# A one-core graph layer on Trainium2: a constant projection transposed in the head, a tile turned inside an accumulation, and a last tile finished in halves

## The chip, the cores and the metric

The kernel runs on one core of a Trainium2 chip. The metric is the device time of one execution in microseconds (us). The core has TensorE (PE, matmuls and transposes into PSUM), VectorE (DVE), ScalarE (ACT), GpSimd (POOL) and SyncE (SP, which only issues DMAs here). ACT and POOL issue some DMAs too. Each engine has its own instruction list, worked off in order; the lists meet only at semaphores.

## The reference

```
h   = relu(layernorm(x))                      # x: 1250 x 512, f32
xn  = batchnorm(h) * g1 + b1
agg = segment_sum(xn[src], dst) / max(deg, 1) # 20000 edges
conv = relu(agg @ W_conv + b_conv)
q, k, v = h @ Wq, h @ Wk, h @ Wv on the first 256 rows, 8 heads of 64
u = (t * scale) @ proj.T                      # proj: 256 x 64, for q and for k
qf, kf = exp(u - diag - max) / 16 + 1e-6
attn = (qf @ (kf.T @ v)) / (qf @ sum(kf)) @ Wo
out = x + batchnorm(conv + attn + h) * g2 + b2
```

## The kernel before, in words

The 1250 rows are ten tiles of 128 (the last has 98), the 512 features four tiles f = 0 to 3. Each engine's order is written out by hand. Eight PSUM banks are given out by two lists, `order` and `order_end`: `pe_open` takes the next name of the list, gives it a bank and waits until that bank's last user has been read; `full` and `landed` are "PE has written it", `read` and `stored` are "it has been read".

**Head (0 to about 27 us).** SP and ACT issue the loads of x, of the edges and of the weights. PE first runs `rouse(18)`, eighteen matmuls on constant ones whose result nobody reads, then `edge_search(0)` (tiny matmuls that count edges, L807), the transposes of h tiles 1 and 0 (L637), one more rouse, `edge_search(1)`, and the matmuls of q (L645). After the transposes of tiles 2 to 5 it runs `project_consts()`: two transposes of the projection `pj` (L818) and one of `vrow`, the five vectors g1, b1, g2, b2, b_conv (L819). Its loads are the last that SP issues before it waits for x tile 7 (L326, L328). DVE copies the result to `pT` and `vec` in `constants()` (L1143, L1144), after the statistics of x and the first piece of batch statistics. On ACT the head is: three x loads (L429), a table load with a first square root (L431), the standard deviation of the first group (L426), h tile 0, the copies of the transposed h tiles 1 and 0 (L389), and then the second group.

**Middle (to 118 us).** Attention, one-hot edge counts, and G = xn @ W_conv (L715), which is split into two f16 parts gh and gl. `uncovered_edges()` loads a flag into PE's registers and branches on it.

**End.** `aggregate(f, c)` (L992) sums gh and gl over ten source tiles s for one column chunk: 20 matmuls. For f = 0 to 2 the chunks are 512, 512 and 226 columns, for f = 3 they are 376, 376, 214, 156 and 128. For each chunk DVE runs `y(f, c)` (L1407, L1412, statistics L1414); after the last chunk `moments` and `scale` give one scale and shift per feature, and ACT scales the tile (L619), as three blocks j. PE turns (transposes) each block (`transpose_z`, L1020), DVE adds x to it (`finish`, L1442), and SP stores it (L345, L349). For f = 2 the blocks 0 and 2 are turned by `turn_with_residual` (x is added by PE, ACT copies the result), and block 1 by `transpose_z` with an add on DVE, all after the last chunk of f = 3. For f = 3 DVE scales block 0 itself (L1461), ACT the rest as 256, 256 and 226 columns; the store of block 1 is issued by ACT (L623), the others by SP.

Of the kernel before, what the change touches and what calls it, by code (L numbers as in the profile page):

```python
# [14 lines left out]
P = 128  # L15
# [26 lines left out]
NPAD = NT * P  # L42
SLOW_LINKS = 8
SEARCHED = 2
ROUSE, ROUSE_NEXT = 18, 1
EP, EJ = 125, E // 125
# [6 lines left out]
def chunks_of(f):  # L53
    return CHUNKS if f < FT - 1 else LAST_CHUNKS


def rows_of(i):
    return P if i < NT - 1 else LAST


def gnn_kernel(nc, x, src, dst, g1, b1, g2, b2, w_conv, b_conv, w_q, w_k, w_v, w_o, proj, out):
    with ExitStack() as ctx:
# [3 lines left out]
        def sem(name):  # L66
# [124 lines left out]

        order = [("first",), ("hT", 1), ("hT", 0), ("q", 0), ("q", 1), ("hT", 2), ("hT", 3), ("hT", 4), ("hT", 5),
# [8 lines left out]
        for f in range(1, FT - 1):  # L201
            order_end += [("agg", f, 0), ("agg", f, 1)] + [("zT", f - 1, j) for j in range(3)] + [("agg", f, 2)]
        order_end += [("agg", FT - 1, c) for c in range(len(LAST_CHUNKS))] + [("zT", FT - 2, j) for j in (0, 2, 1)]
        order_end += [("zT", FT - 1, j) for j in range(3)]
        uses = {}
# [103 lines left out]
        @block.sync  # L309
        def _(sp):  # L310
            def load_x(i):
                sp.dma_start(xs[0:rows_of(i), i, :], x[i * P:i * P + rows_of(i), :]).then_inc(x_in[i], 16)

            load_x(0)
            sp.dma_start(edst[:, :], dst.rearrange("(p j) -> p j", p=EP)).then_inc(dst_in, 16)
            wq_rows = w_q.rearrange("(t p) n -> p t n", p=P)
            sp.dma_start(wq[:, :, 0:2 * P], wq_rows[:, :, 0:2 * P]).then_inc(wq_in[0], 16)
            load_x(2)
            load_x(4)
            sp.dma_start(wq[:, :, 2 * P:D], wq_rows[:, :, 2 * P:D]).then_inc(wq_in[1], 16)  # L320
            for i in (6, 7, 8, 9):
                if i == NT - 1:
                    sp.wait_ge(pad_zero, 1)
                load_x(i)
            for k, v in enumerate((g1, b1, g2, b2, b_conv)):
                sp.dma_start(vrow[4 * k:4 * k + 4, :], v.rearrange("(t p) -> t p", p=P)).then_inc(vec_in, 16)  # L326
            for k in range(2):
                sp.dma_start(pj[:, :, k * DH:(k + 1) * DH], proj.rearrange("(t p) d -> p t d", p=P)).then_inc(pj_in, 16)  # L328
            sp.wait_ge(x_in[7], 16)
            sp.dma_start(wk, w_k.rearrange("(t p) n -> p t n", p=P)).then_inc(wk_in, 16)  # L330
            sp.dma_start(wc[:, :, :], w_conv.rearrange("(t p) n -> p t n", p=P)).then_inc(wc_in, 16)
            sp.dma_start(wvo[:, :, :], w_v.rearrange("(t p) n -> p t n", p=P)).then_inc(wv_in, 16)
            for t in range(AT):
                landed(sp, "v", t)
            sp.dma_start(wvo[:, :, :], w_o.rearrange("(t p) n -> p t n", p=P)).then_inc(wo_in, 16)
            sp.dma_start(esrc[:, :], src.rearrange("(p j) -> p j", p=EP)).then_inc(src_in, 16)
            landed(sp, "agg", 0, 0)
            for i in range(NT):
                load_x(i)
            for f in range(FT):  # L340
                c = slice(f * P, (f + 1) * P)
                for j in {FT - 2: (0, 2, 1), FT - 1: (0, 2)}.get(f, (0, 1, 2)):
                    stored(sp, "zT", f, j)
                    if j < 2:
                        sp.dma_start(out[512 * j:512 * (j + 1), c].rearrange("(t p) n -> p t n", p=P),  # L345
                                     xs[:, 4 * j:4 * (j + 1), c]).then_inc(o_out, 16)
# [4 lines left out]
            sp.wait_ge(o_out, 16 * 4 * FT)  # L351

# [31 lines left out]
        def _(act):  # L384
# [42 lines left out]

            for i in (1, 3, 5):
                act.dma_start(xs[:, i, :], x[i * P:(i + 1) * P, :]).then_inc(x_in[i], 16)  # L429
            act.wait_ge(cst_set, 7)  # L430
# [4 lines left out]
            store_hT(1, ACT.Relu)  # L435
            store_hT(0)
            ln_std_of(1)
            act.wait_ge(ln_ready, 2)
# [182 lines left out]
            c = slice((FT - 1) * P, D)  # L621
            stored(act, "zT", FT - 1, 1)
            act.dma_start(out[512:1024, c].rearrange("(t p) n -> p t n", p=P), xs[:, 4:8, c]).then_inc(o_out, 16)  # L623
# [3 lines left out]
        def _(pe):  # L627
# [133 lines left out]

            def uncovered_edges():
                pe.wait_ge(flag_ready, 1)
                covered = pe.value_load(flag[0:1, 0:1], min_val=0, max_val=1)
                with pe.If(covered == 0):
# [90 lines left out]

            rouse(ROUSE)
            edge_search(0)
            pe.wait_ge(id_set, 1)
            transpose_h(1)  # L860
# [12 lines left out]
            transpose_h(5)  # L873
            project_consts()
            pe.wait_ge(wk_in, 16)
# [102 lines left out]
            for i in range(2):  # L978
                stored(pe, "attnT", i)
            heads_out(0)  # L980
            heads_out(1)
            uncovered_edges()
            assert counts[0] == NGRP

            def aggregate(f, c):
                c0, cn = chunks_of(f)[c]
                pe.wait_ge(group_stored, -(-(c0 + cn) // (GW * W)))
                acc = pe_open(pe, "agg", f, c)
                for s in range(NT):
                    n = rows_of(s)  # L990
                    for gg in (gh, gl):
                        last = nc.tensor.matmul(acc[:, 0:cn], gg[0:n, s, f * P:(f + 1) * P], A16[0:n, s, c0:c0 + cn],  # L992
                                                start=(s == 0 and gg is gh), stop=(s == NT - 1 and gg is gl))
                last.then_inc(full("agg", f, c), 1)
# [12 lines left out]
            def transpose_z(f, parts=(0, 1, 2)):  # L1007
                for j in parts:
                    acc = pe_open(pe, "zT", f, j)
                    if f < FT - 1:  # L1010
                        pe.wait_ge(z_act, 3 * f + j + 1)
                    elif j == 0:
                        pe.wait_ge(z_dve, 1)
                    elif j == 2:
                        pe.wait_ge(z_act, 3 * f + 3)
                    for i in range(4 * j, min(4 * j + 4, NT)):
                        if f == FT - 1 and i in (4, 6):
                            pe.wait_ge(z_act, 3 * f + i // 2 - 1)
                        o = (i - 4 * j) * P
                        last = nc.tensor.transpose(acc[:, o:o + P], yT[:, f, i * P:(i + 1) * P], ident[:, :])  # L1020
                    last.then_inc(full("zT", f, j), 1)
# [18 lines left out]
            turn_with_residual(FT - 2, 2)  # L1040
            transpose_z(FT - 2, (1,))
            transpose_z(FT - 1)


        @block.vector
        def _(dve):
# [94 lines left out]
            def constants():  # L1141
                acc = landed(dve, "consts")
                V.tensor_copy(pT[:, :], acc[:, 0:M])  # L1143
                V.tensor_copy(vec[:, :], acc[:, M:M + 20]).then_inc(read("consts"), 1)  # L1144
                stored(dve, "consts")
# [241 lines left out]
            def last_phase(slow):  # L1387
# [47 lines left out]
                def finish(f, j):  # L1435
                    a, b = 4 * j, min(4 * j + 4, NT)
# [17 lines left out]
                f = FT - 1  # L1454
                for c in range(len(LAST_CHUNKS) - 1):
                    y(f, c)
# [3 lines left out]
                dve.wait_ge(st2_ready, FT)  # L1460
                V.tensor_scalar(yT[:, f, 0:512], yT[:, f, 0:512], s2[:, f:f + 1], t2[:, f:f + 1],  # L1461
                                ALU.mult, ALU.add).then_inc(z_dve, 1)
                finish(f - 1, 1)
                for j in range(3):
                    finish(f, j)
# [79 lines left out]
```

## Time and profile before

| what | value |
|---|---|
| median of 3 runs | 175.11 us (174.8 to 175.3) |
| the profiled execution, its own time | 174.95 us |
| its span, first to last instruction | 173.1 us |
| mean granted TensorE clock | 0.992 |
| busy: PE, DVE, ACT, POOL | 166.0, 138.3, 89.8, 7.6 us |

The profiled time is 1.85 us above its span; that part lies outside the instructions. A matmul's busy time overlaps its neighbours', so PE's 166.0 us say that it was never long without work, not that it ran at its peak.

### The profile page before, as it was taken

The numbers are of one execution on the slowest core, as the hardware profiler recorded it, in microseconds if no ns is written. First come the engines' busy times: TensorE is split into PE (matmuls) and PEld (weight loads), VectorE is DVE, ScalarE is ACT, GpSimd is POOL, SyncE is SP. The second block draws the span as 40 slices with busy tenths as digits, with TensorE's granted clock in tenths as the row PEclk, the third lists the DMA queues.
The fourth block names the chain that finished last, engine by engine and source line by source line (L and its number), as shares of the span: only waits on it lengthen the run. The fifth ranks groups of instructions, "written<-read, shape, count | busy, mean of one in ns | idle before, by whom it ended". The sixth has DMA issues, their size and how long they took to land.

```text
span 173.1 us, 3035 instructions
## 1 busy us (share of the span) xinstructions
PE 166.0 (96%) x1135; PEld 109.6 (63%) x1136; DVE 138.3 (80%) x317; ACT 89.8 (52%) x163; POOL 7.6 (4%) x22
## 2 busy tenths in 40 slices
PE   7999999999999999999999999999999999999980
PEld 2588887545545546557767797684464574777960
DVE  3987989899947786999656785976999998597980
ACT  3228998749793789969506164218600505004060
POOL 5047000000000000000000000000000000000000
PEclk9999999999999999999999999999999999999996
DMA  5999960000800000000000000000395004050046
GB/s 169 353 342 284 310 221 0 0 4 0 251 12 0 4 0 0 0 4 2 0 4 0 0 4 0 0 4 4 94 315 187 0 27 121 6 146 2 0 118 183
DMA packets 12412, 13.71 MB, mean 79 GB/s; under 512 B 1474, under 2 KB 7788, under 8 KB 12396
## 3 DMA queue, kind: packets, MB, share of 16 engines
q1 hardware_dynamic: 11116, 12.18, 22.4%
q10 hardware_dynamic: 960, 1.05, 1.8%
q0 software_dynamic: 320, 0.26, 0.7%
q8 instruction: 11, 0.18, 0.4%
q14 instruction: 5, 0.04, 0.1%
HBM read 10.92 MB, written 2.56 MB: 78 GB/s over the span
## 4 chain that ended last, share of the span: by engine, by line
PE 88%; DVE 6%; ACT 2%; issue 1%; DVEq 0%; ACTq 0%
PE bank L992 22%; PE bank L715 20%; PE bank L645 8%; PE bank L666 4%; PE bank L739 4%; PE bank L729 4%; PE bank L758 4%; PE bank L797 4%; PE bank L692 4%; PE bank L657 3%; PE bank L637 3%; PE bank L703 2%; PE bank L1020 2%; DVE r L1412 1%; DVE r L1407 1%
## 5 line engine op out<-in xcount | busy, mean ns | idle before, releaser
L992 PE MATMUL bank<-r,gh 128*128 128x512 f16 (+8 forms) x140 | 39.3, 314 | 0.0
L992 PE MATMUL bank<-r,gl 128*128 128x512 f16 (+8 forms) x140 | 39.3, 313 | 0.0
L715 PE MATMUL bank<-wc,xs 128*128 128x512 f32 (+1 forms) x80 | 38.5, 608 | 0.2 <-DVE gl L1243 0.2
L1100 DVE TENSOR_TENSOR ohb<-iota,bcol 128x1280 f16<-128x1280 f16 x25 | 20.5, 819 | 3.7 <-PE bank L657 3.7
L715 PEld LDWEIGHTS bank<-wc,xs 128*128 128x128 f32 (+1 forms) x80 | 13.6, 187 | 11.6 <-issue 11.6
L398 ACT ACTIVATE r<-bank 128x500 f16<-128x500 f32 x25 | 18.3, 765 | 3.4 <-PE bank L657 3.4
L992 PEld LDWEIGHTS bank<-r,gh 128*128 128x128 f16 (+1 forms) x140 | 13.5, 97 | 8.5 <-issue 0.3
L992 PEld LDWEIGHTS bank<-r,gl 128*128 128x128 f16 (+1 forms) x140 | 13.6, 97 | 8.2
L613 ACT ACTIVATE bw<-mv,epst 128x1 f32<-128x1 f32 x4 | 1.2, 295 | 31.0 <-DVE mv L1418 31.0
L645 PE MATMUL bank<-hT,r 128*128 128x256 f32 x64 | 14.6, 383 | 0.0
L657 PEld LDWEIGHTS bank<-ohv,ohb 128*128 128x128 f16 x250 | 9.7, 98 | 6.6 <-issue 5.3
L521 ACT ACTIVATE gh<-bank 128x512 f16<-128x512 f32 (+1 forms) x10 | 6.0, 601 | 14.6 <-PE bank L715 14.6
L645 PEld LDWEIGHTS bank<-hT,r 128*128 128x128 f32 x64 | 11.9, 189 | 2.0 <-issue 0.4
L1243 DVE SCALAR_TENSOR_TENSOR gl<-bank,gh 128x512 f16<-128x512 f32 (+1 forms) x10 | 6.9, 688 | 5.2 <-ACT gh L521 5.2
L1407 DVE SCALAR_TENSOR_TENSOR r<-bank,cinv,r 128x512 f32<-128x512 f32 (+5 forms) x14 | 8.2, 584 | 3.3 <-PE bank L992 3.2
L1100 DVE TENSOR_TENSOR ohv<-iota,vcol 128x500 f16<-128x500 f16 x25 | 10.3, 413 | 0.0
L657 PE MATMUL bank<-ohv,ohb 128*128 128x50 f16 x250 | 10.3, 184 | 0.0
L619 ACT ACTIVATE r<-r,t,s 128x512 f32<-128x512 f32 (+2 forms) x12 | 7.5, 689 | 3.0 <-DVE t L1432 3.0
L1412 DVE SCALAR_TENSOR_TENSOR r<-r,nb,hT 128x512 f32<-128x512 f32 (+5 forms) x14 | 8.3, 591 | 0.5
L729 PEld LDWEIGHTS bank<-v,r 128*128 128x128 f32 x64 | 7.6, 192 | 1.0 <-issue 1.0
L797 PE MATMUL bank<-cone 128*128 128x512 f16 x19 | 6.9, 536 | 1.2 <-DVE cone L1062 1.2
L1393 DVE RECIPROCAL r<-r 128x1250 f32<-128x1250 f32 x1 | 8.0, 7967 | 0.1
(179 smaller groups left out, 269.1 us busy)
## 6 DMA issues: line engine op xcount, KB each, us to landing
xs<-in_x SPq DMA_DIRECT2D x15, 256.0 KB, 5.0
out<-xs SPq DMA_DIRECT2D x7, 256.0 KB
r<-in_L_gnn_Wq SPq DMA_DIRECT2D x2, 512.0 KB, 7.2
r<-in_L_gnn_Wk SPq DMA_DIRECT2D x1, 1024.0 KB, 5.6
wc<-in_L_gnn_W_conv SPq DMA_DIRECT2D x1, 1024.0 KB, 9.6
wvo<-in_L_gnn_Wv SPq DMA_DIRECT2D x1, 1024.0 KB, 12.8
wvo<-in_L_gnn_Wo SPq DMA_DIRECT2D x1, 1024.0 KB, 5.2
xs<-in_x ACTq DMA_DIRECT2D x3, 256.0 KB, 4.4
```

What stands on the lines that cost most here:

```text
L398: act.activation(A16[:, :, p * GW * W:(p + 1) * GW * W].rearrange("p a (q d) -> p q a d", q=GW), bank[p % 2][:, 0:GW * NT * W].rearrange(" ...
L619: act.activation(yT[:, f, a:b], yT[:, f, a:b], ACT.Identity, bias=t2[:, f:f + 1], scale=s2[:, f:f + 1]).then_inc(z_act, 1)
L645: last = nc.tensor.matmul(acc[:, t * NA:(t + 1) * NA], w[:, f, c:c + P], hT[:, f, 0:NA], start=(f == 0), stop=(f == FT - 1))
L657: last = nc.tensor.matmul(bank[p % 2][:, q * NT * W:(q + 1) * NT * W], ohb[:, s, :], ohv[:, s, :], start=True, stop=True)
L715: last = nc.tensor.matmul(acc[0:n, :], xnT[:, f, i * P:i * P + n], wc[:, f, :], start=(f == 0), stop=(f == FT - 1))
L729: last = nc.tensor.matmul(acc[:, j * (DH + 1):(j + 1) * (DH + 1)], kf[:, t, h, m * P:(m + 1) * P], v1[:, t, h, :], start=(t == 0), stop=(t ...
L797: nc.tensor.matmul(bank[0][:, :], cone[:, :], cone[:, 0:1].to_broadcast([P, 512]), start=True, stop=True)
L992: last = nc.tensor.matmul(acc[:, 0:cn], gg[0:n, s, f * P:(f + 1) * P], A16[0:n, s, c0:c0 + cn], start=(s == 0 and gg is gh), stop=(s == NT ...
L1100: last = V.tensor_tensor(oh[:, s0:s0 + n, :].rearrange("p s (m t) -> p s m t", t=2), iota16[:, 0:size].rearrange("p (m t) -> p m t", t=2). ...
L1393: link(V.reciprocal(rdeg[:, :], rdeg[:, :]))
L1407: V.scalar_tensor_tensor(out=yT[:, f, c0:c0 + cn], in0=sums, scalar=cinv[:, f:f + 1], in1=rdeg[:, c0:c0 + cn], op0=ALU.mult, op1=ALU.mult) ...
L1412: link(V.scalar_tensor_tensor(out=yT[:, f, c0:c0 + cn], in0=yT[:, f, c0:c0 + cn], scalar=nb[:, f:f + 1], in1=hT[:, f, c0:c0 + cn], op0=ALU ...
```

## The change

It moves the projection's transposes to the head of PE's list and turns the rest around them, and it rearranges the end of f = 2 and f = 3.

- **Head.** `rouse` runs 15 instead of 18 matmuls; `project_consts()` follows at once, ahead of `edge_search(0)`. Its loads (five of `vrow`, two of `pj`) are issued by ACT behind x tile 1; x tiles 3 and 5 go to SP's queue, ahead of 2 and 4. ACT copies the result to `pT` and `vec` behind the copy of h tile 0; DVE's two copies go.
- **Bank lists.** `consts` is first in `order`; block 1 of f = 2 stands between chunks 1 and 2 of f = 3 in `order_end`, and f = 3 has four blocks.
- **Flag.** The load of the flag into PE's registers stands ahead of `heads_out(1)`, the branch stays.
- **Block 1 of f = 2** is turned inside chunk 1 of f = 3, ahead of source tile 7; DVE adds x to it between chunks 0 and 1, and SP stores it first of the three.
- **f = 3** has the blocks (0, 2), (2, 4), (4, 8), (8, 10) in tiles: DVE scales, PE turns, DVE finishes and SP stores the first 512 columns as two halves.

```diff
-ROUSE, ROUSE_NEXT = 18, 1
+TURN_AT = 7
+ROUSE, ROUSE_NEXT = 15, 1
+def tiles_of(f, j):
+    if f < FT - 1:
+        return 4 * j, min(4 * j + 4, NT)
+    return ((0, 2), (2, 4), (4, 8), (8, NT))[j]
...
-        order = [("first",), ("hT", 1), ("hT", 0), ("q", 0), ("q", 1), ("hT", 2), ("hT", 3), ("hT", 4), ("hT", 5),
-                 ("consts",), ("k", 0), ...
+        order = [("consts",), ("first",), ("hT", 1), ("hT", 0), ("q", 0), ("q", 1), ("hT", 2), ("hT", 3), ("hT", 4), ("hT", 5),
+                 ("k", 0), ...
-        order_end += [("agg", FT - 1, c) for c in range(len(LAST_CHUNKS))] + [("zT", FT - 2, j) for j in (0, 2, 1)]
-        order_end += [("zT", FT - 1, j) for j in range(3)]
+        order_end += [("agg", FT - 1, c) for c in range(2)] + [("zT", FT - 2, 1)]
+        order_end += [("agg", FT - 1, c) for c in range(2, len(LAST_CHUNKS))]
+        order_end += [("zT", FT - 2, j) for j in (0, 2)]
+        order_end += [("zT", FT - 1, j) for j in range(4)]
...  # SP
-            load_x(2)
-            load_x(4)
+            for i in (3, 5, 2, 4):
+                load_x(i)
-            for k, v in enumerate((g1, b1, g2, b2, b_conv)):
-                sp.dma_start(vrow...)
-            for k in range(2):
-                sp.dma_start(pj...)
-                for j in {FT - 2: (0, 2, 1), FT - 1: (0, 2)}.get(f, (0, 1, 2)):
+                for j in {FT - 2: (1, 0, 2), FT - 1: (0, 1, 3)}.get(f, (0, 1, 2)):
...  # ACT
-            for i in (1, 3, 5):
-                act.dma_start(xs[:, i, :], ...)
+            act.dma_start(xs[:, 1, :], ...)
+            for k, v in enumerate((g1, b1, g2, b2, b_conv)):
+                act.dma_start(vrow...)
+            for k in range(2):
+                act.dma_start(pj...)
             store_hT(0)
+            acc = landed(act, "consts")
+            act.activation(pT[:, :], acc[:, 0:M], ACT.Copy)
+            act.activation(vec[:, :], acc[:, M:M + 20], ACT.Copy).then_inc(read("consts"), 1)
...  # PE
             rouse(ROUSE)
+            pe.wait_ge(id_set, 1)
+            project_consts()
             edge_search(0)
-            project_consts()
             heads_out(0)
+            pe.wait_ge(flag_ready, 1)
+            covered = pe.value_load(flag[0:1, 0:1], min_val=0, max_val=1)
             heads_out(1)
                 for s in range(NT):
+                    if (f, c, s) == (FT - 1, 1, TURN_AT):
+                        transpose_z(FT - 2, (1,))
             turn_with_residual(FT - 2, 2)
-            transpose_z(FT - 2, (1,))
-            transpose_z(FT - 1)
+            transpose_z(FT - 1, (0, 1, 2, 3))
...  # DVE
-                V.tensor_copy(pT[:, :], acc[:, 0:M])
-                V.tensor_copy(vec[:, :], acc[:, M:M + 20]).then_inc(read("consts"), 1)
+                y(f, 0)
+                finish(f - 1, 1)
+                for c in range(1, len(LAST_CHUNKS) - 1):
                     y(f, c)
-                V.tensor_scalar(yT[:, f, 0:512], ...)
-                finish(f - 1, 1)
-                for j in range(3):
+                for a in (0, 256):
+                    V.tensor_scalar(yT[:, f, a:a + 256], ...).then_inc(z_dve, 1)
+                for j in range(4):
                     finish(f, j)
```

## Rows read from the trace of the kernel before

**Rows 1.** The page: the chain that ended last, shares of the span by engine

```profile
PE 88%; DVE 6%; ACT 2%; issue 1%; DVEq 0%; ACTq 0%
```

**Rows 2.** The chain in order of time, the head (start us, us, what)

```profile
1.21 6.56 PE bank L797 x18
7.77 0.18 PE bank L807 x4
...
9.97 7.02 PE bank L645 x32
...
18.73 0.22 PE bank L818 x2
...
19.12 3.65 PE bank L645 x16
```

**Rows 3.** Windows of L797: stretch, length, PE and PEld busy, PEclk, DMA share, GB/s

```profile
1.20:5.80 4.60, 4.59 (x11) 1.65 (x12) 1.00 0.81 250
6.30:7.60 1.30, 1.30 (x7) 0.49 (x5) 1.00 1.06 384
```

**Rows 4.** Timeline of ACT, head (start us, us, instruction, idle before)

```profile
0.76 1.39 ACTq L429 DMA_DIRECT2D xs<-in_x  x3
2.18 1.28 ACT L431 ACT_TABLE_LOAD   x1 [2.18 <-issue]
...
5.58 0.29 ACT L426 ACTIVATE lnw<-mv,epst 128x2 f32<-128x2 f32 x1 [1.90 <-DVE mv L1072]
...
12.21 0.30 ACT L426 ACTIVATE lnw<-mv,epst 128x4 f32<-128x4 f32 x1 [2.64 <-DVE mv L1072]
```

**Rows 5.** L429, ACT's three loads of x: from issue to landing

```profile
DMA to landing us min/median/max: 3.5/4.4/6.4
```

**Rows 6.** Timeline of SP's queue: the last vector load and both projection loads

```profile
7.32 0.29 SPq L326 DMA_DIRECT2D vrow<-in_L_gnn_b_conv  x1
7.66 0.91 SPq L328 DMA_DIRECT2D pj<-in_L_gnn_proj  x2
```

**Rows 7.** L328, the two projection loads: from issue to landing

```profile
DMA to landing us min/median/max: 6.4/6.8/7.2
```

**Rows 8.** Timeline of DVE, head: statistics of x tiles 3 and 5; copy to pT

```profile
8.52 1.28 DVE L1068 BATCH_NORM_STATS2 st<-xs 128x6 f32<-128x512 f32 x2
...
21.07 0.41 DVE L1143 COPY pT<-bank 128x256 f32<-128x256 f32 x1
```

**Rows 9.** L764, the flag load on PE's sequencer (duration ns, start us)

```profile
L764 PEldq TENSOR_LOAD <-flag x1: 486/486/486, 113.5 to 113.5; - x1
```

**Rows 10.** The chain in order of time, from the turn of f = 1 on

```profile
149.59 1.09 PE bank L1020 x10
...
166.09 0.56 DVE r L1461
```

**Rows 11.** Timeline of DVE, end: chunk 1 of f = 3; the last adds

```profile
159.04 0.61 DVE L1407 SCALAR_TENSOR_TENSOR r<-bank,cinv,r 128x376 f32<-128x376 f32 x1 [1.02 <-PE bank L992]
...
167.44 1.62 DVE L1442 TENSOR_TENSOR xs<-bank,xs 128x512 f32<-128x512 f32 x3 [0.21 <-PE bank L1020]
```

**Rows 12.** L1442, DVE's four last adds (ns min/median/max)

```profile
L1442 DVE TENSOR_TENSOR xs<-bank,xs x4: 416/683/692, 166.5 to 168.7; 128x512 f32<-128x512 f32 x3, 128x256 f32<-128x256 f32 x1
```

**Rows 13.** Timeline of ACT, end: the scalings of f = 2 and f = 3

```profile
156.31 1.99 ACT L619 ACTIVATE r<-r,t,s 128x512 f32<-128x512 f32 x3 [1.00 <-DVE t L1432]
...
166.38 1.55 ACT L619 ACTIVATE r<-r,t,s 128x256 f32<-128x256 f32 x3
```

**Rows 14.** Timeline of SP's queue, end

```profile
167.36 1.18 SPq L345 DMA_DIRECT2D out<-xs  x2
169.09 0.84 SPq L349 DMA_DIRECT2D out<-xs  x2
```

**Rows 15.** Windows, end: length; PE, PEld, DVE, ACT, POOL busy, PEclk, DMA share, GB/s

```profile
168.50:169.50 1.00, 0.00 (x0) 0.00 (x0) 0.57 (x2) 0.00 (x0) 0.00 (x0) 1.00 0.99 284
...
170.50:171.50 1.00, 0.00 (x0) 0.00 (x0) 0.00 (x0) 0.00 (x0) 0.00 (x0) 0.50 0.95 253
```

More of the change, by code:

```diff
@@ L324, in _ @@
                 load_x(i)
-            for k, v in enumerate((g1, b1, g2, b2, b_conv)):
-                sp.dma_start(vrow[4 * k:4 * k + 4, :], v.rearrange("(t p) -> t p", p=P)).then_inc(vec_in, 16)
-            for k in range(2):
-                sp.dma_start(pj[:, :, k * DH:(k + 1) * DH], proj.rearrange("(t p) d -> p t d", p=P)).then_inc(pj_in, 16)
             sp.wait_ge(x_in[7], 16)
@@ L341, in _ @@
                 c = slice(f * P, (f + 1) * P)
-                for j in {FT - 2: (0, 2, 1), FT - 1: (0, 2)}.get(f, (0, 1, 2)):
+                for j in {FT - 2: (1, 0, 2), FT - 1: (0, 1, 3)}.get(f, (0, 1, 2)):
                     stored(sp, "zT", f, j)
-                    if j < 2:
-                        sp.dma_start(out[512 * j:512 * (j + 1), c].rearrange("(t p) n -> p t n", p=P),
-                                     xs[:, 4 * j:4 * (j + 1), c]).then_inc(o_out, 16)
+                    a, b = tiles_of(f, j)
+                    if b < NT:
+                        sp.dma_start(out[a * P:b * P, c].rearrange("(t p) n -> p t n", p=P), xs[:, a:b, c]).then_inc(o_out, 16)
                     else:
@@ L350, in _ @@
             sp.wait_ge(src_in, 16)
-            sp.wait_ge(o_out, 16 * 4 * FT)
+            sp.wait_ge(o_out, 16 * (4 * FT + 1))
         @block.gpsimd
@@ L426, in ln_std_of @@
                 act.activation(lnw[:, 1, a:b], mv[:, a:b, 1], ACT.Sqrt, bias=epst[:, 0:1]).then_inc(ln_std, 1)
-            for i in (1, 3, 5):
-                act.dma_start(xs[:, i, :], x[i * P:(i + 1) * P, :]).then_inc(x_in[i], 16)
+            act.dma_start(xs[:, 1, :], x[P:2 * P, :]).then_inc(x_in[1], 16)
+            for k, v in enumerate((g1, b1, g2, b2, b_conv)):
+                act.dma_start(vrow[4 * k:4 * k + 4, :], v.rearrange("(t p) -> t p", p=P)).then_inc(vec_in, 16)
+            for k in range(2):
+                act.dma_start(pj[:, :, k * DH:(k + 1) * DH], proj.rearrange("(t p) d -> p t d", p=P)).then_inc(pj_in, 16)
             act.wait_ge(cst_set, 7)
@@ L621, in _ @@
             c = slice((FT - 1) * P, D)
-            stored(act, "zT", FT - 1, 1)
+            stored(act, "zT", FT - 1, 2)
             act.dma_start(out[512:1024, c].rearrange("(t p) n -> p t n", p=P), xs[:, 4:8, c]).then_inc(o_out, 16)
@@ L760, in heads_out, with uncovered_edges @@
                 last.then_inc(full("ha", i), 1)
-            def uncovered_edges():
-                pe.wait_ge(flag_ready, 1)
-                covered = pe.value_load(flag[0:1, 0:1], min_val=0, max_val=1)
+            def uncovered_edges(covered):
                 with pe.If(covered == 0):
@@ L857, in _ @@
             rouse(ROUSE)
+            pe.wait_ge(id_set, 1)
+            project_consts()
             edge_search(0)
-            pe.wait_ge(id_set, 1)
             transpose_h(1)
@@ L980, in _ @@
             heads_out(0)
+            pe.wait_ge(flag_ready, 1)
+            covered = pe.value_load(flag[0:1, 0:1], min_val=0, max_val=1)
             heads_out(1)
-            uncovered_edges()
+            uncovered_edges(covered)
             assert counts[0] == NGRP
@@ L1008, in transpose_z @@
                 for j in parts:
+                    a, b = tiles_of(f, j)
                     acc = pe_open(pe, "zT", f, j)
@@ L1011, in transpose_z @@
                         pe.wait_ge(z_act, 3 * f + j + 1)
[L1012 to L1017, printed above, removed]
+                    elif j < 2:
+                        pe.wait_ge(z_dve, j + 1)
+                    for i in range(a, b):
+                        if f == FT - 1 and i in (4, 6, 8):
                             pe.wait_ge(z_act, 3 * f + i // 2 - 1)
-                        o = (i - 4 * j) * P
+                        o = (i - a) * P
                         last = nc.tensor.transpose(acc[:, o:o + P], yT[:, f, i * P:(i + 1) * P], ident[:, :])
@@ L1141, in constants @@
             def constants():
-                acc = landed(dve, "consts")
-                V.tensor_copy(pT[:, :], acc[:, 0:M])
-                V.tensor_copy(vec[:, :], acc[:, M:M + 20]).then_inc(read("consts"), 1)
                 stored(dve, "consts")
@@ L1435, in finish @@
                 def finish(f, j):
-                    a, b = 4 * j, min(4 * j + 4, NT)
+                    a, b = tiles_of(f, j)
                     c = slice(f * P, (f + 1) * P)
@@ L1454, in last_phase @@
                 f = FT - 1
-                for c in range(len(LAST_CHUNKS) - 1):
+                y(f, 0)
+                finish(f - 1, 1)
+                for c in range(1, len(LAST_CHUNKS) - 1):
                     y(f, c)
@@ L1460, in last_phase @@
                 dve.wait_ge(st2_ready, FT)
-                V.tensor_scalar(yT[:, f, 0:512], yT[:, f, 0:512], s2[:, f:f + 1], t2[:, f:f + 1],
-                                ALU.mult, ALU.add).then_inc(z_dve, 1)
-                finish(f - 1, 1)
-                for j in range(3):
+                for a in (0, 256):
+                    V.tensor_scalar(yT[:, f, a:a + 256], yT[:, f, a:a + 256], s2[:, f:f + 1], t2[:, f:f + 1],
+                                    ALU.mult, ALU.add).then_inc(z_dve, 1)
+                for j in range(4):
                     finish(f, j)
```

2 rows, old and new, of the table order are left out of this document.

## The prediction, on record before the changed kernel ran

> **What bounds the kernel now.** I read the chain that ended last first, because it says whose time counts. PE holds 88% of it [rows 1]. Followed in order of time, the chain stays on PE from 1.21 us nearly without a hole through the head [rows 2], and it leaves PE for DVE only when the second chunk of f = 3 lands at 159.04 [rows 11]. From there DVE's work on the chunks, the scale and the last blocks sets the end [rows 10, 11], and behind it the stores. So a PE instruction in the head or in the aggregation counts in full, a DVE or ACT instruction before 159 us counts only if PE waits for it, and after 159.04 it is the other way round. Then I read ACT's, DVE's and SP's timelines in the head [rows 4, 6, 8] and the landings of their loads [rows 5, 7], since the change makes PE wait for loads that have long landed today. Last come the end's timelines [rows 11, 13, 14] and the DMA engines' share there [rows 15].
>
> **Head, what goes.** Three rousing matmuls go. The first eleven take 4.6 us, so 0.42 us apart; in the stretch from 6.3 us on seven records fill 1.3 us, under 0.22 us apart [rows 3]: that is PE at 1.2 GHz and then at 2.4 GHz, and it rose after some five microseconds of rousing. The three that go are fast ones: 18 took 6.56 us, 15 end at 1.21 + 6.56 - 3 x 0.217 = 7.12 us. The three transposes of the constants took 19.12 - 18.73 = 0.39 us on the path [rows 2]. They are moved, not removed: their place at 18.73 closes up by 0.39 us and the head opens by as much. Without a wait, then, the head is 0.65 us shorter and all of it reaches the end of PE's unbroken chain.
>
> **Head, the wait that is added.** PE now stands still until all five vector loads and both projection loads have landed, and behind the waiting instruction are both edge searches, the h transposes and the q matmuls; behind those, ACT's copies of h and DVE's first_rows, with the gathers that POOL issues after it. When do the loads land? ACT issues x tile 1 at 0.76; one x load takes 0.46 us of its queue [rows 4]. A vector load takes 0.29 and a gap of 0.05, a projection load 0.46 [rows 6]. So the five vectors are issued from 1.22 to 2.92, the projection at 2.92 and 3.38. How long a load needs from issue to landing depends on what is ahead of it: 3.5 us for the first x on ACT's queue, 4.4 for the second, 6.4 for the third [rows 5], 6.4 and 7.2 for the projection itself behind SP's whole list [rows 7]. The bounds for the second projection load are thus 3.38 + 3.5 = 6.9 us and 3.38 + 7.2 = 10.6 us. Its case is nearest to the second x on ACT's queue, one large transfer ahead and the bus shared with SP's: 3.38 + 4.4 = 7.8 us. PE then waits from 7.12 to 7.8; with 0.05 us to wake and 0.39 us of transposes, edge_search(0) starts at 8.24 where it started at 7.77 [rows 2]. That is 0.47 us late, minus the 0.39 us at 18.73: **the head costs 0.08 us** (bounds: -0.65 with the landing by 7.1, and 10.6 + 0.05 + 0.39 - 7.77 - 0.39 = +2.9 with the latest).
>
> The second x of ACT's queue, issued at 1.2, landed 4.4 us later [rows 4, 5]: its own queue didn't spare it the traffic. The Trainium skill, "DMA: Bandwidth & Descriptors", section "Issuing engines are not separate DMA queues", says as much: DMAs of all issuers run on the same 16 engines and interleave, and a second issuer saves issue time only. By it the move to ACT buys no bandwidth, and the projection's wait must be read from loads that ran in the same crowd.
>
> **Head, the edits that I cost at nothing.** ACT's issues end at about 3.85 instead of 2.15, its table load of 1.28 us [rows 4] at 5.2 and the first square root at 5.4; the standard deviation is wanted at 5.58. The cover is only 0.2 us thick; without it, the first group's scale is late by as much. ACT's two new copies, some 0.4 and 0.2 us, fall into its 2.64 us of idle time before 12.21 [rows 4]. DVE loses about 0.5 us of copies at 21.07 [rows 8], but PE waited for nothing of DVE's there, so this is slack and not time. x tiles 3 and 5 now queue behind half of Wq on SP; DVE wants them from 8.52 on [rows 8], and since the same bytes are on the same engines in another order, I expect them by about 8. If one were late, tiles 2 to 5 of h would be. The third place is the k matmuls, which follow at once where the constants stood: their weights wait for x tile 7, but no longer behind seven small loads. The flag's load was done at 113.5, under the matmuls that PE still had queued [rows 9]; the load wasn't what PE waited for at the branch, so moving it gives nothing.
>
> **End, the turn inside the chunk.** Ten transposes of f = 1 took 1.09 us between two chunks [rows 10], so four take 0.44. They stand ahead of chunk 1's last six matmuls, and DVE idles 1.02 us for that chunk before 159.04 [rows 11]. So the landing moves to 159.48 and everything behind it, in full: **+0.44 us**. Their operand is ready in time: ACT's second block of f = 2 is done two thirds into 156.31 + 1.99 [rows 13], near 157.8, and source tile 7 of the chunk comes up at about 157.9. DVE's added add (0.68 us [rows 12]) fits between chunk 0 and the 159.48. What is taken away at the end is worth little: the turn ran while DVE scaled, and the add while PE turned block 0; DVE idled 0.21 us even so [rows 11].
>
> **End, the halves.** The scale of 512 columns takes 0.56 us [rows 10], so half some 0.35; PE starts 0.2 us earlier and turns two blocks instead of four, 0.22 us less, and DVE's first add can start near 167.0 instead of 167.44. But ACT's three scalings end at 166.38 + 1.55 = 167.93 [rows 13] whatever DVE does, and the last two adds hang on them: the 128x512 add starts perhaps 0.08 us earlier, the last (416 ns [rows 12]) follows it. **-0.07 us** (bounds 0 and -0.15, the last add's start at 168.65 against 167.93 and 0.57 us for wake-up and two transposes).
>
> **End, the stores.** SP issues the store of block 1 of f = 2 at 167.36 [rows 14] in the middle of the last rush; after, it goes out near 160. The DMA engines are full in that rush (share 0.99 at 284 GB/s, 0.95 at 253 [rows 15]), and 256 KB are 0.92 us of their time. SP's last issue starts near 169.48 and ends at 169.93 [rows 14]; the span ends at 173.1. An unloaded 256 KB load takes 3.5 us, of which 0.9 are its bytes, so a small one needs some 2.6; the last store's 3.1 leave about 0.5 to gain, and the one ACT issues just before it has its queue freed too. I take **-0.6 us** (bounds 0, if latency alone sets the end, and -0.92). One more SP issue falls between 167.4 and 169.0, where SP has nothing else.
>
> **Sum.** 174.95 + 0.08 + 0.44 - 0.07 - 0.6 = 174.80 us for the profiled execution. That one is 0.16 us under the median of the three runs, so the median to expect is 174.96, say 174.9. Less than 0.3% (0.53 us) either way is about what a measurement of this kernel can't tell from no change.
>
> **The rivals.** (a) The projection lands early. If it is there by 7.1, PE never waits and the head gives its whole 0.65 us: 175.11 - 0.65 - 0.23 = 174.2. For it: ACT's queue has only one x ahead of the projection, and 128 KB are half of one x tile. Against: the share of the bus it got in its neighbours' time. Any landing under 7.4 us makes the kernel faster by over 0.3%. (b) The other side: the projection is late. Its pieces are small, and its own loads took 6.4 and 7.2 us [rows 7]; at a landing of 8.8 us the head costs 1.08 us and the kernel takes 176.0; at the 6.4 us of the third x [rows 5] it is 9.8 us and 176.9. It decides from 8.5 us on. (c) PE's idle time costs the clock: PE rose to 2.4 GHz only shortly before the wait begins [rows 3], and at the end of the kernel, idle after its last transposes, it is granted 0.50 by 170.5 [rows 15]. If it fell in the new gap, rousing it again at 0.42 instead of 0.22 us a matmul would cost about 12 x 0.2 = 2.4 us: 177.5. The gap of 0.7 us is shorter than what preceded that fall, 2 us. The Trainium skill, "TensorE: Matmul & The Clock Gate", section "HAM oscillation — how this bites in real kernels", warns of just this: PE that waits for a DMA between bursts drops to the low clock. (d) The stores gain nothing: 175.5, still no change.
>
> **Chances.** My forecast with (d), within 0.3%: 0.41. (a), faster: 0.37. (b) 0.18 and (c) 0.04, slower: 0.22. The range: down to 173.9, where (a) and the full 0.92 us of the stores meet (175.11 - 0.65 - 0.55); up to 176.0, where (b) has its middle price; (c) and the far half of (b) are left out.
>
> **What would show it.** In the profile after: 15 rousing matmuls ending at 7.1, and PE's idle time ahead of L818, 0 (a), 0.7 (mine) or over 1.3 us (b); the granted clock and the spacing of the q matmuls; q's start against 9.97; the k matmuls' start; DVE's wait for chunk 1 with 0.44 us more on the clock than the head's shift; the last add; and the time from SP's last issue to the end of the span, 3.1 before and some 2.5 after. I would be wrong by another way if x tile 3 or 5 came late for DVE, or if ACT's table load pushed the first square root beyond 5.6.

## The result, and the profile after

The changed kernel takes **183.75 us** (median of 4 runs, 183.61 to 184.04), against 175.11 us before: ratio **1.050, interval 1.048 to 1.052**. I had predicted 174.9 us and given slower a chance of 0.22. The profiled execution took 183.61 us with a span of 180.9 us, 7.8 us longer than before. Its time outside the span is 2.7 us where it was 1.85. This part isn't the change's doing as far as the runs show: in the changed kernel's own executions it lay between 2.0 and 2.8 us, in the unchanged kernel's later ones between 1.8 and 2.3, and in those of a kernel with only the flag's load moved up to 2.9. So the spans are compared below. The changed kernel's other executions have spans of up to 182.0 us and lower granted clocks (0.956 to 0.965, against the profiled 0.971), so the account below holds for the profiled one.

The page of the kernel after (busy time, the granted clock in 40 slices, the chain by engine):

```profile
PE 169.6 (94%) x1133; PEld 112.2 (62%) x1133; DVE 138.5 (77%) x317; ACT 90.0 (50%) x165; POOL 7.6 (4%) x22
...
PEclk9955799999999999999999999999999999999999
...
PE 83%; DVE 6%; DMA 5%; ACT 2%; ACTq 2%; issue 1%; DVEq 0%
```

Before, no DMA was named in the chain's shares [rows 1]; now one has 5% of it, and the clock is down to a half in slices 3 and 4. The timeline of PE in the head and the chain through the same stretch say which DMA it is (after; start us, us):

```profile
1.21 5.99 PE L806 MATMUL bank<-cone 128*128 128x512 f16 x15 [1.21 <-DVE cone L1073]
11.97 0.66 PE L827 MATMUL bank<-ident,pj 128*128 128x128 f32 x2 [4.77 <-DMA pj<-in_L_gnn_proj]
```

```profile
3.68 8.16 DMA pj<-in_L_gnn_proj
...
11.97 0.66 PE bank L827 x2
12.63 0.22 PE bank L828
12.85 0.52 PE bank L816 x4
13.37 1.81 PE bank L648 x8
15.18 0.43 PE bank L806
15.60 1.60 PE bank L816 x16
17.21 8.51 PE bank L656 x32
25.72 1.75 PE bank L648 x16
...
125.70 0.53 PE bank L1038 x3
126.23 19.33 PE bank L1005 x100
```

PE stood still for 4.77 us: the second projection load, issued at 3.68, landed 8.16 us later at 11.84. And what follows is slow. The eight transposes of h take 1.81 us (0.93 before), sixteen edge matmuls 1.60 (0.87), the 32 matmuls of q 8.51 instead of 7.02 [rows 2]. Windows of the kernel after (stretch, length, PE, PEld, DVE, ACT, POOL busy, PEclk, DMA share, GB/s):

```profile
7.20:9.80 2.60, 0.00 (x0) 0.00 (x0) 2.55 (x4) 0.51 (x1) 0.00 (x0) 1.00 1.07 375
10.00:12.00 2.00, 0.03 (x1) 0.06 (x1) 0.00 (x0) 0.00 (x0) 0.00 (x0) 0.50 1.10 359
12.00:17.00 5.00, 5.00 (x32) 4.37 (x33) 0.00 (x0) 1.55 (x4) 0.00 (x0) 0.50 0.71 219
17.00:20.00 3.00, 3.00 (x9) 2.46 (x10) 2.25 (x11) 0.30 (x1) 1.56 (x2) 0.50 1.01 372
20.20:22.00 1.80, 1.80 (x10) 1.58 (x9) 1.73 (x6) 1.22 (x2) 1.50 (x2) 1.00 1.03 397
```

PE went idle at 7.20. The clock was still granted in full at 9.8, was at 0.50 (1.2 GHz) from 10.0, and stayed there for eight more microseconds after PE was busy again, until 20.1.

**The account of the span.** The first transpose of the constants stands where edge_search(0) stood: it starts 11.97 - 7.77 = 4.20 us later. That is the wait of 4.77 us, less the 0.57 us by which rousing ended earlier (7.20 against 7.77). The transposes' own 0.39 us are only moved to the front, away from 18.73. From there to the end of q's matmuls PE took 25.72 - 11.97 = 13.75 us; before, the same instructions took 0.39 + (16.99 - 7.77) = 9.61 us, so the low clock cost +4.14. Then it comes back in steps. The aggregation begins 7.66 us late (126.23 against 118.57): of the 8.34 us, the flag's load takes back 0.5 and the first k matmuls, 3.46 us instead of 3.65, 0.2. DVE's wait for chunk 1 ends 8.20 late (+0.54, the turn), DVE's last add 8.13 late (-0.07), the span 7.8 (-0.3, the stores).

### The profile page after: what moved, and what is told of

It is laid out like the page before. It is cut to its first block, busy times and chain, and to the rows that moved or that the text cites. A ratio compares the mean times of both kernels' runs of the same rounds, so it can differ in the third digit from the quotient of the medians.

```text
span 180.9 us, 3034 instructions
## 1 busy us (share of the span) xinstructions
PE 169.6 (94%) x1133; PEld 112.2 (62%) x1133; DVE 138.5 (77%) x317; ACT 90.0 (50%) x165; POOL 7.6 (4%) x22
## 4 chain that ended last, share of the span: by engine, by line
PE 83%; DVE 6%; DMA 5%; ACT 2%; ACTq 2%; issue 1%; DVEq 0%
PE bank L1005 21%; PE bank L726 19%; PE bank L656 9%; DMA pj<-in_L_gnn_proj 5%; PE bank L677 4%; PE bank L750 4%; PE bank L740 4%; PE bank L769 4%; PE bank L703 4%; PE bank L668 3%; PE bank L648 3%; PE bank L1032 2%; PE bank L714 2%; PE bank L816 1%; ACTq L435 1%; DVE r L1420 1%
## 5 line engine op out<-in xcount | busy, mean ns | idle before, releaser
L726 PEld LDWEIGHTS bank<-wc,xs 128*128 128x128 f32 (+1 forms) x80 | 13.6, 187 | 11.6 <-issue 11.6
L1005 PEld LDWEIGHTS bank<-r,gl 128*128 128x128 f16 (+1 forms) x140 | 13.6, 97 | 8.1
L656 PE MATMUL bank<-hT,r 128*128 128x256 f32 x64 | 16.0, 409 | 0.0
L656 PEld LDWEIGHTS bank<-hT,r 128*128 128x128 f32 x64 | 13.0, 207 | 2.4 <-issue 0.4
L394 ACT ACTIVATE hT<-bank 128x512 f32<-128x512 f32 (+1 forms) x10 | 5.2, 590 | 8.7 <-PE bank L648 8.7
## 6 DMA issues: line engine op xcount, KB each, us to landing
wvo<-in_L_gnn_Wv SPq DMA_DIRECT2D x1, 1024.0 KB, 10.9
```

The costliest lines, as they stand in the source:

```text
L656: last = nc.tensor.matmul(acc[:, t * NA:(t + 1) * NA], w[:, f, c:c + P], hT[:, f, 0:NA], start=(f == 0), stop=(f == FT - 1))
L726: last = nc.tensor.matmul(acc[0:n, :], xnT[:, f, i * P:i * P + n], wc[:, f, :], start=(f == 0), stop=(f == FT - 1))
```

## Experiments

Each ran beside the kernel before on the same chip; the ratios are against that. They are the record's, each with its 95% interval, and can differ from the quotient of the two medians by 0.1 to 0.2%. "Span" and the lines shown are the profiled execution's.

### The end's part alone

```diff
 # head as in the kernel before; kept of the change:
+                    if (f, c, s) == (FT - 1, 1, TURN_AT):
+                        transpose_z(FT - 2, (1,))
...  # the halves of f = 3, the stores' order, the flag's load ahead of heads_out(1)
```

> The kernel before with the end's part of the change and the flag's load moved, the head untouched. Theory 1, the whole loss is in the head: 174.8 us, from 175.11 with -0.5 (the flag: in the profile after, the gap ahead of the degree matmuls is gone), +0.54 (the four transposes inside chunk 1), -0.07 and -0.3 (stores). Theory 2, the 0.85 us by which the changed kernel's time grew beyond its span comes from the end: 175.6 us.

Measured: 174.73 us against 175.45, ratio **0.997 (0.995 to 0.998)**, span 172.8. So the loss is in the head, and the end's part with the flag is a small gain. DVE's end (timeline of this run):

```profile
158.39 0.69 DVE L1451 TENSOR_TENSOR xs<-bank,xs 128x512 f32<-128x512 f32 x1 [0.61 <-PE bank L1030]
159.35 0.61 DVE L1416 SCALAR_TENSOR_TENSOR r<-bank,cinv,r 128x376 f32<-128x376 f32 x1 [0.27 <-PE bank L1003]
...
167.40 1.91 DVE L1451 TENSOR_TENSOR xs<-bank,xs 128x256 f32<-128x256 f32 x4 [0.27 <-PE bank L1030]
```

The add that was moved (158.39) fits into the hole ahead of chunk 1, as predicted. From the start of the aggregation (118.34 here, 118.57 before) to chunk 1 on DVE it is 41.01 us against 40.47: +0.54.

### The constants' transposes back in their old place, loads still on ACT

```diff
-            pe.wait_ge(id_set, 1)
-            project_consts()
             edge_search(0)
+            pe.wait_ge(id_set, 1)
...
             transpose_h(5)
+            project_consts()
```

> The changed kernel with the constants' transposes and their copies on ACT back behind the transposes of h tile 5; the loads stay on ACT's queue, ROUSE stays 15. Theory 1, PE's wait for the loads and what it does to the clock is the loss: 174.2 us (174.8 less three rousing matmuls, 0.65), q starts near 9.4. Theory 2, the loads' new order on the queues (x tiles 3 and 5 on SP, small loads on ACT) costs by itself: 176 us or more.

Measured: 175.47 against 175.45, ratio 1.001 (0.998 to 1.004), span 173.5; two of its ten executions took 178.8 and 179.1 us, with a granted clock of 0.984. In the profiled one the wait and the low clock are gone, so waiting for these loads in this place makes the loss. But it is 1.3 us above my 174.2 (0.9 if the kernel before is taken at the 175.45 measured beside it), and its span is 0.7 us longer than that of the end's part alone, which has three rousing matmuls more. PE's and ACT's timelines and the chain show where that goes:

```profile
1.21 4.73 PE L806 MATMUL bank<-cone 128*128 128x512 f16 x15 [1.21 <-DVE cone L1073]
...
7.84 1.06 PE L648 MATMUL bank<-ident,xs 128*128 128x128 f32 x8 [1.54 <-DVE xs L1118]
...
19.89 0.48 PE L656 MATMUL bank<-hT,r 128*128 128x256 f32 x1 [0.75 <-DMA r<-in_L_gnn_Wk]
```

```profile
5.85 0.28 ACT L431 ACTIVATE lnw<-mv,epst 128x2 f32<-128x2 f32 x1
```

```profile
6.05 8.33 DMA xs<-in_x
14.38 0.02 issue
14.40 5.44 DMA r<-in_L_gnn_Wk
```

The h transposes cannot start before DVE has scaled x tile 1 (L1118), so removing three rousing matmuls saves nothing: q's matmuls start at 9.85, against 9.83 before. Here this scale is itself late. ACT's seven small issues push its table load back, the standard deviation starts at 5.85 instead of 5.5, and the transposes start at 7.84, against 7.58 in the end's part alone. That is the danger the prediction named for ACT's edits, at 0.25 us. And x tile 7 lands at 14.4, so SP issues Wk later than before (12.48), and PE waits 0.75 us for it. How much of that delay is the small loads' doing isn't shown: over all profiled executions SP issued Wk at 12.5 to 13.8 us with the head's loads as before, and at 13.0 to 14.4 with the changed ones, and in the split kernel further below, with no vector ahead of the x tiles, at 13.6.

### Rousing until the projection lands

```diff
-ROUSE, ROUSE_NEXT = 15, 1
+ROUSE, ROUSE_NEXT = 37, 1
```

> The changed kernel with 37 rousing matmuls instead of 15, so that PE works until the projection lands near 11.9 us. Theory 1, the loss has two parts, 4.85 us of waiting and 4.15 us of work at the low clock behind it: 179.6 us, with q's first 32 matmuls back at 7.0 us. Theory 2, the low clock is not the gap's doing: 183.7 us.

Measured: 178.93 us, ratio **1.019 (1.017 to 1.022)**, span 177.1. The projection lands as late as before (12.02), and 22 more matmuls whose result nobody reads buy back 3.8 us of span. They end at 10.9; the gap of 1.24 us that is left doesn't lower the clock. The chain of this run:

```profile
12.02 0.14 issue
12.15 0.41 PE bank L827 x2
...
13.05 0.93 PE bank L648 x8
...
15.07 7.02 PE bank L656 x32
```

Same landing, same instructions, full clock: 9.9 us from 12.15 to 22.09 where the changed kernel took 13.75. So the long gap brings the low clock, and that is about half of the loss of span.

### The projection ahead of the vectors on ACT's queue

```diff
-            for k, v in enumerate((g1, b1, g2, b2, b_conv)): act.dma_start(vrow...)
             for k in range(2): act.dma_start(pj...)
+            for k, v in enumerate((g1, b1, g2, b2, b_conv)): act.dma_start(vrow...)
```

> The changed kernel with the two projection loads issued ahead of the five vector loads on ACT's queue. Theory 1, the five small loads in front are what keeps the projection's first packet back: the projection is in by 8.5 us and PE waits for the vectors at the latest until 10, 178 to 181 us. Theory 2, the share of the bus is the cause: the last landing stays at 11.8 us and the time at 183.7 us.

Measured: four executions from 175.93 to 181.34 us, too unlike for a ratio; granted clock 0.994 in the shortest and 0.964 in the longest, which is the profiled one (span 178.8). Its tile view has the projection at 3.9 and 5.4 us from issue to landing, so it was in at 7.1. The vectors, 2 KB each and the last of them issued at 3.9, kept PE until 9.15:

```profile
9.15 0.66 PE L827 MATMUL bank<-ident,pj 128*128 128x128 f32 x2 [2.42 <-DMA vrow<-in_L_gnn_b_conv]
```

Theory 1 holds for the landing. The profiled execution works at half the clock from 9.0 to 19.1. The granted clocks suggest that this kernel loses the clock in some executions and not in others, which goes with the spread of 5 us; only the one trace shows it.

### The same with rousing until the vectors land

```diff
-ROUSE, ROUSE_NEXT = 15, 1
+ROUSE, ROUSE_NEXT = 27, 1
```

> The changed kernel with the projection loads ahead of the vectors' (as in the run with that order) and 27 rousing matmuls instead of 15, so that PE is busy until the last vector lands near 9.1 us. Theory 1, the low clock comes from the gap even at 2.4 us: 176.3 us (174.7 for the end's part, +1.9 for the later start of the edge search, -0.39 for the closed place), all runs alike. Theory 2, the gap alone is the cost and 2.4 us do not lower the clock: no better than 180 us.

Measured: 176.75 us (176.44 to 177.07), ratio 1.008 (1.006 to 1.011), span 175.0; PE busy in all 13 us from 7 to 20, clock 1.00. The spread is gone with the gap. Rousing went on until 10.12, about 1 us longer than the vectors would have asked. q starts at 12.85, 2.9 us late, and the kernel is 1.3 us over the one before.

### The constants split: the projection alone in the head

```diff
             act.dma_start(xs[:, 1, :], ...)
-            for k, v in enumerate((g1, b1, g2, b2, b_conv)): act.dma_start(vrow...)   # back to SP, behind x tile 9
             for k in range(2): act.dma_start(pj...)
...
             transpose_h(5)
+            turn_vectors()   # the transpose of vrow; DVE copies it to vec
```

> The changed kernel with the constants split: only the projection is loaded on ACT's queue behind x tile 1 and turned in the head; the five vector loads go back to SP's queue, where they were, and their transpose back behind h tile 5 (ACT no longer copies it, DVE does). Theory 1, the five small loads are what holds the projection and PE up: the projection lands by 7.5 us, PE waits under 0.5 us, the clock stays up, ratio 0.996 to 1.002. Theory 2, the projection's own small pieces on a full bus are slow: it lands after 9 us and the ratio is over 1.02.

Measured: 175.04 against 175.40, ratio 1.000 (0.997 to 1.002), span 173.2; one of its twelve executions took 179.75 us, with a granted clock of 0.98. PE's timeline, and the tile view of the projection:

```profile
1.22 4.98 PE L805 MATMUL bank<-cone 128*128 128x512 f16 x15 [1.22 <-DVE cone L1077]
7.80 0.41 PE L825 MATMUL bank<-ident,pj 128*128 128x128 f32 x2 [1.60 <-DMA pj<-in_L_gnn_proj]
...
19.60 2.64 PE L655 MATMUL bank<-hT,r 128*128 128x256 f32 x11 [0.27 <-DMA r<-in_L_gnn_Wk]
```

```profile
DMA to landing us min/median/max: 3.9/4.9/6.0
```

Without the five vector loads the projection is in at 7.7 us, not 11.84, and the loss is gone. It was issued at 1.7 and took 6.0 us to land. PE still idles 1.6 us (here the clock had risen early and rousing ended at 6.2), and in this execution the clock stayed. But a projection in the head is worth nothing either: its ratio is no better than that of the end's part alone (0.995 to 0.998). Whether it is worse isn't shown, since the intervals overlap.

### What ten kilobytes in front of the projection do

Two runs on the split kernel. One puts x tile 3 (256 KB), taken from SP's queue, between x tile 1 and the projection on ACT's queue, the other one vector (2 KB); the other four vectors stay with SP.

```diff
             act.dma_start(xs[:, 1, :], ...)
+            act.dma_start(xs[:, 3, :], ...)        # first run; SP then loads x tiles 5, 2, 4
+            act.dma_start(vrow[0:4, :], g1...)     # second run
             for k in range(2): act.dma_start(pj...)
```

> The run with the split constants (vectors back on SP's queue), with x tile 3 moved from SP's queue to ACT's, between x tile 1 and the projection: 256 KB in front of the projection in the place where the changed kernel has 10 KB in five loads. Theory 1, it is the number of small loads that holds ACT's ring, not their bytes: the projection lands earlier than the changed kernel's 11.84 us, near 9 us, and PE waits some 2.5 us. Theory 2, the bytes in front and the full bus set it: 11 us or later.

> The run with the split constants, with one of the five vector loads (g1, 2 KB) on ACT's queue between x tile 1 and the projection. Theory 1, each small load holds the ring by itself: the projection lands near 8.5 us, a fifth of the way from 7.7 (no vector in front) to 11.84 (five). Theory 2, only the sum of issue times counts, 0.35 us a load: 8.0 us.

Measured: 180.72 us, ratio 1.031 (1.027 to 1.036), with the tile; 178.30 us, 1.018 (1.014 to 1.021), with one vector. PE's timelines, first the run with the tile, then that with one vector:

```profile
9.71 0.66 PE L826 MATMUL bank<-ident,pj 128*128 128x128 f32 x2 [3.05 <-DMA pj<-in_L_gnn_proj]
```

```profile
9.74 0.66 PE L826 MATMUL bank<-ident,pj 128*128 128x128 f32 x2 [2.68 <-DMA pj<-in_L_gnn_proj]
```

| in front of the second projection load, behind x tile 1 | issued | landed | issue to landing |
|---|---|---|---|
| nothing (split) | 1.7 us | 7.7 us | 6.0 us |
| x tile 3, 256 KB | 2.2 | 9.6 | 7.4 |
| one vector, 2 KB | 2.2 | 9.6 | 7.4 |
| five vectors, 10 KB (the changed kernel) | 3.7 | 11.84 | 8.2 |

Each row is one profiled execution; the changed kernel's landing came back at 12.02 in the run with 37 rousing matmuls. Bytes don't set it: 2 KB hold the projection back as much as 256 KB do, 1.4 us beyond the half microsecond of issue time, and theory 2 of the second run falls. Theory 1 of the first is right in direction; the landing is 9.6, not 9. The fifth of the way that I gave for one vector was too little, since the first costs most: five cost 4.1 us in all, 2.0 of issue time and 2.2 of queue. The record of single DMA packets in the same traces, which the views above don't print, shows the queue working in order. Without a vector in front, the projection's packets start at 3.46 us and the last at 7.23. With one vector, its four packets start at 3.86 to 4.03 and the projection's at 4.87 to 8.96. In the changed kernel the five vectors' twenty packets take from 3.95 to 7.08, and the projection's first packet starts only at 7.26, its last at 11.21. Why twenty packets of 512 bytes take three microseconds stays open. Windows of the two runs show the low clock for different lengths; the first three lines are the tile's, the last three the vector's:

```profile
10.00:12.00 2.00, 2.00 (x13) 2.00 (x12) 0.00 (x0) 0.32 (x1) 0.00 (x0) 0.50 1.08 373
12.00:14.00 2.00, 2.00 (x17) 1.74 (x16) 0.00 (x0) 1.15 (x3) 0.00 (x0) 0.50 0.74 222
14.00:16.00 2.00, 2.00 (x9) 1.73 (x10) 1.37 (x5) 0.00 (x0) 0.55 (x1) 0.50 0.70 165
```

```profile
10.00:12.00 2.00, 2.00 (x13) 2.00 (x12) 0.00 (x1) 0.29 (x1) 0.00 (x0) 0.50 1.09 369
12.00:14.00 2.00, 2.00 (x21) 1.74 (x20) 0.06 (x1) 1.18 (x3) 0.00 (x0) 0.75 0.83 276
14.00:16.00 2.00, 2.00 (x10) 1.74 (x10) 1.90 (x9) 0.00 (x0) 1.17 (x1) 1.00 0.43 100
```

PE restarts at 9.7 in both; one is back at 2.4 GHz near 13, the other only after 18, and that is most of the 2.4 us between them.

### The flag's load alone

```diff
             heads_out(0)
+            pe.wait_ge(flag_ready, 1)
+            covered = pe.value_load(flag[0:1, 0:1], min_val=0, max_val=1)
             heads_out(1)
-            uncovered_edges()
+            uncovered_edges(covered)
```

> The kernel before with one edit: the flag's load into PE's registers stands ahead of heads_out(1). Theory 1: the branch takes some 3.35 us of PE's sequencer whatever it waits for, and starts 0.8 us earlier when the load is out of its way, so the hole ahead of the degree matmuls closes: -0.5 us, ratio 0.997, degree matmuls start right behind the last head matmul. Theory 2, the load is hidden and the hole is the branch itself (as my prediction had it): ratio 1.000.

Measured: 174.72 against 175.40, ratio **0.998 (0.996 to 0.999)**, span 172.7. The branch on PE's sequencer and the chain behind it, first before (L765), then in this run (L763):

```profile
L765 PEldq COMPARE_BRANCH  x1: 3347/3347/3347, 114.4 to 114.4; - x1
...
117.54 0.34 issue
117.88 0.69 PE bank L1026 x3
```

```profile
L763 PEldq COMPARE_BRANCH  x1: 3476/3476/3476, 113.5 to 113.5; - x1
...
117.57 0.53 PE bank L1026 x3
```

The branch takes as long whether it starts early or late. Before, it started behind the load at 114.4 and ended at 117.72, after the last head matmul (117.54); now it ends at 117.02, and the degree matmuls follow at 117.57 without a hole (117.88 and a hole of 0.34 before). The aggregation starts 0.47 us earlier.

### The end's part without the turn inside the chunk

```diff
-                    if (f, c, s) == (FT - 1, 1, TURN_AT):
-                        transpose_z(FT - 2, (1,))
...
             turn_with_residual(FT - 2, 2)
+            transpose_z(FT - 2, (1,))
...  # add and store back as well; halves and flag stay
```

> The run with the end's part alone, with block 1 of f = 2 back behind the last chunk (turn, add and store where they were); the halves and the flag's load stay. Theory 1, the turn inside chunk 1 costs 0.54 us of PE on the path and gives back about 0.5 us by the earlier store: same time as the end's part alone, ratio 0.997, with the last issue 0.5 us earlier and the landing behind it 0.5 us longer. Theory 2, the stores' queue matters less than the path: 0.5 us faster than the end's part alone, ratio 0.994.

Measured: 174.70 against 175.40, ratio 0.997 (0.995 to 0.999), span 172.9: no difference from the flag alone (0.998) or from the end's part alone (0.997). SP's queue, first this run, then the end's part alone:

```profile
167.02 3.11 SPq L353 DMA_DIRECT2D out<-xs  x3
170.18 0.97 SPq L356 DMA_DIRECT2D out<-xs  x2
```

```profile
159.11 7.40 SPq L355 DMA_DIRECT2D out<-xs  x2
...
167.85 0.89 SPq L355 DMA_DIRECT2D out<-xs  x2
169.34 0.83 SPq L358 DMA_DIRECT2D out<-xs  x2
```

The line of 7.40 us spans two stores, block 1 at 159.11 and block 0 at 166.13, each issued in 0.38 us; the other line of x3 holds three stores in a row. DVE's last add ends at 168.59 here and at 169.31 there; 0.18 us of that is an earlier start of the aggregation. But here one of the three stores takes 1.78 us to issue and the next 0.86, where the stores of L355 and L358 there take 0.35 to 0.47 each, and SP's last issue ends at 171.15, not 170.17. With the flag alone, where the last add ends at the same time (168.58) and there is one store less, SP's last issue ends at 169.45. So the halves' added store seems to eat here what the shorter path gave. The turn, which sends one store early, avoids that at the price of 0.54 us of path.

### Wk one tile earlier

```diff
-            sp.wait_ge(x_in[7], 16)
+            sp.wait_ge(x_in[6], 16)
             sp.dma_start(wk, ...)
```

> The run with the end's part alone, with SP's wait ahead of the load of Wk on x tile 6 instead of x tile 7. In that run's trace PE waited for Wk at 19.3 us, 0.2 us behind its own readiness. Theory 1, Wk sets the start of the k matmuls: it lands 0.5 us earlier, PE starts at 19.1, ratio to the kernel before 0.995. Theory 2, Wk only takes the bus from x tiles 8 and 9 and from the vectors: no gain over the end's part, ratio 0.997 or above.

Measured: 174.45 against 175.09, ratio 0.996 (0.994 to 0.998), span 172.8. The fastest version tried, and faster than both kernels, but its interval overlaps that of the end's part alone, and in its trace the k matmuls start at 19.41, no earlier than that run's 19.31. Wk was issued at 12.09 instead of 13.36 and PE no longer waited for it, but q's matmuls had started half a microsecond later in this execution, since rousing took 6.59 us and not 5.45. Whether Wk's edit gives anything stays open.

## Why the prediction was wrong

- **The landing of the second projection load is the step that failed**: "Its case is nearest to the second x on ACT's queue ... 3.38 + 4.4 = 7.8 us". It landed at 11.84, 1.2 us beyond the latest bound I had. It was issued at 3.68, and from there it took 8.2 us where I had put 4.4. The runs split that: even with nothing but x tile 1 in front it takes 6.0, and the five vector loads, which I had counted by their issue time alone, add 2.2: the projection's packets wait behind theirs. The bound from the projection's own rows [rows 7] failed too: 7.2 us is not the most that such a load can take. PE's matmuls began 0.14 us after the landing, where I had put 0.05 from no row.
- **The clock's rival (c) was right in kind and far too cheap in chance** (0.04). I priced it for a gap of 0.7 us, and a gap of that size indeed kept the clock (0.74 us in the end's part alone), but I never joined it to a late landing, although the two are one event. Late landing and low clock together cost 4.2 + 4.1 us. The Trainium skill, "TensorE: Matmul & The Clock Gate", section "HAM oscillation — how this bites in real kernels", describes just this pair, a DMA wait and then work at the low clock; the trace agrees, 4.77 us idle and 0.50 granted until after 20 us.
- **"The head is 0.65 us shorter" without a wait was wrong**: the h transposes wait for DVE's scale of x tile 1 (7.5 to 7.8 us in the runs where PE waited for it), which the rousing matmuls only covered. An early landing, rival (a), could have put the constants' 0.39 us into that hole, but the k matmuls would then have met another wait: in the changed kernel Wk was issued at 13.88 and took 5.3 us, so it landed at 19.2, and before they started at 19.12. By these rows (a) would have gained nothing; that is my estimate, since no run had so early a landing.
- **Wk behind x tile 7**: I took it that Wk would come no later. In the changed kernel that cost nothing, since PE reached the k matmuls at 27.47. In runs whose head is fast PE waits for Wk: 0.27 us in the split kernel, 0.75 with the place undone, but also 0.43 in the end's part alone, whose loads are those of before. So it is a limit that stood close behind PE already; that the moved loads tighten it isn't shown.
- **The flag at nothing was wrong**: the load was hidden, but the branch behind it was not, and it took 3.35 us before. It gives 0.5 us, and it is the one part of the change that is shown to pay.
- **The turn, +0.44**: right in mechanism, 0.54 measured. **The halves, -0.07**: right, -0.07. **The stores, -0.6**: right in kind, too large. From the end of SP's last issue to the end of the span it was 3.2 us before, 2.6 in the end's part alone and 2.85 in the changed kernel, so -0.3 to -0.5. Counted from DVE's last add (4.0, 3.5 and 3.7 us) it is the same.

## What to carry to other kernels

Before a wait is put at the front of an engine's list, count the transfers ahead of the awaited one, not only their bytes: here one 2 KB load in front cost as much as a 256 KB tile, and the second of two loads of 64 KB took 6 us on a full bus. Price a wait in the head of TensorE together with the clock that it may cost, and if the wait can't be shortened, cover it: 22 more useless matmuls gave 3.8 us back. Better still, take off its queue what stands ahead of the awaited load: without the five vectors the loss was gone. And an instruction that is hidden may still hold up the one behind it: look where the branch ends, not where the load does.

## What the runs showed of the hardware that I had not expected

- PE's gap and the clock, by the profiled executions: kept after gaps of 1.24, 1.54 and 1.60 us, lost after 2.42, 2.68, 3.05 and 4.77 us. These are single executions, and no line between them is shown: of the two kernels with gaps of 1.54 and 1.60 us, 3 of 22 executions ran some 4 us longer with a granted clock of 0.98, and the shortest execution of the one with 2.42 us had 0.994. The gaps of those executions weren't recorded. With PE busy again, the clock stayed at 1.2 GHz for some 3 us of work in one run and for 8 to 10 in the others.
- The branch on TensorE's sequencer takes 3.3 to 3.8 us over the thirteen profiled programs, wherever it starts, while a branch on DVE's sequencer took 0.06 us in the same traces (L1469). Why they differ no run shows.
- Small loads hold ACT's queue: one of 2 KB adds 1.4 us to the next load's way from issue to landing, five add 2.2.
- SP's issue of a store can itself take long in the last rush: 1.78 us for one and 0.86 for the next in the kernel with halves and no turn inside the chunk, where a store before takes 0.34 to 0.45.
